# Channel attention on one core: the tensor engine takes the 49 taps two at a time

## The chip, the cores and the metric

The program runs on one NeuronCore of a Trainium2 chip. It is one launch of four layers over a tensor of 4 x 256 x 64 x 64 in float32. The metric is the device time in microseconds, and lower is better. Five engines work side by side, each on its own queue in strict program order: PE (TensorE, with its weight loads), DVE (VectorE), ACT (ScalarE), POOL (GpSimd) and SP (SyncE, which here only issues transfers). They meet at semaphores: an instruction waits until a counter has reached a value, and the instructions behind it on its engine wait with it.

## What is computed

Only layer 2 is touched. For each channel and each pixel it weighs a 7 x 7 window of values by a softmax over the products of the channel's query with the window's keys. There are 49 taps.

```python
def _L2_conv_ref(x, w_q, w_k, w_v, rel_h, rel_w):        # K = 7, PAD = 3
    q = jnp.einsum('bchw,oc->bohw', x, w_q)
    kmap = jnp.einsum('bchw,oc->bohw', x_pad, w_k)
    vmap = jnp.einsum('bchw,oc->bohw', x_pad, w_v)
    kwin = _unfold2d(kmap, K)
    vwin = _unfold2d(vmap, K)
    kwin = jnp.concatenate([kwin[:, :half] + rel_h, kwin[:, half:] + rel_w], axis=1)
    ...
    attn = jax.nn.softmax(q[..., None] * kwin, axis=-1)
    out = jnp.sum(attn * vwin, axis=-1)
    return out
```

The input x is the group-normalised output of layer 1, and `out` is added to it.

## The kernel before

`channel_attention` (line 1395) is a program written by hand: one function per engine lists all its instructions, and semaphores tie the queues. The image is cut into bands of 16 rows, 16 in all (n, counted from 0). A band has four **tiles** (t = 0 to 3) of 128 channels x 512 pixels: `tile_of` makes tiles 0 and 1 of the first half of the channels and tiles 2 and 3 of the second. Each tile runs over 49 **taps** (j). All engines walk through the same order of bands, tiles and taps.

What each engine does for a tap:

- DVE, `multiply` (L1998): key plus relative bias, times the query, into one of three PSUM banks, `stage`. It waits until ACT has emptied that bank, that is for the exponential of three taps ago. Tap 1 of a band's first tile waits for that of tap 48 before it (`bank_lag` 2).
- PE, `shift` (L1679): one matmul of 512 columns with minus the identity takes off the upper bound `top` of the exponents. It waits for the multiply (`multiplied`).
- ACT, `exponential` (L1847): stage to `se` in SBUF. It waits for the shift.
- POOL, `weigh` (L1909): `se` times the window of values into `ev`, 3 or 4 taps in one instruction.
- PE, `sum_exponential` and `sum_weighted` (both through `add_up`, L1686): four transposing matmuls of 128 columns each add a tap of `se` to the bank `pe_sum`, or a tap of `ev` to the bank `pv_sum`. The first comes `E_LAG` = 2 taps behind the shift, the second `V_LAG` = 12 taps.

In between stand works of other tiles. The projections of the next half-band (K1, K2, Q1, Q2 in tiles 0 and 2, V1, V2 in tiles 1 and 3; K0 and V0 only where an image begins) are put on PE by `PROJ_AT`, in two halves g at taps j and j + 1. All use the one bank `pj`. ACT copies each out two taps after its place (L1821), and DVE takes the new keys out of `pj` too (L1946, L1950), to make the running maxima and minima `near` (L1958) from which `ext`, `high` and `top` come (L1974, L1981, L1983). `NEAR` and `EXT_AT` say at which taps.

The end of a tile runs into the next one. ACT takes `pe_sum` after the exponential of tap 1 (`take_e_sums`, L1835), DVE inverts it in four pieces at taps 3, 5, 7 and 9 (L2006), and divides `pv_sum` after its multiply of tap 12 (`divide`, L2014), for which it needs the weighted sum of tap 48. For that reason the weighted sum of tap 0 (`late`) stands behind the shift of tap 12. PE turns the quotient back at tap 20 (`back`, L1720), DVE adds it to x at tap 23 (L2022). ACT places the next tile's query after the exponential of tap 46 (`place_query`, L1828), when all multiplies of the tile are done.

Of the kernel before, what the change touches and what calls it, by code (L numbers as in the profile page):

```python
# [1389 lines left out]
NTAP = K2 * K2  # L1390
# [4 lines left out]
def channel_attention(nc, sems, x_in, coef, x_out, stats, w_t, rel, ident_in, zeros):  # L1395
# [3 lines left out]
    with ctx:  # L1399
# [68 lines left out]
        E_LAG, V_LAG = 2, 12  # L1468
# [22 lines left out]
        def tiles(n, t, per, more):  # L1491

            return n * (TPB * per) + (t * per + more)
# [5 lines left out]
        def parts(H):  # L1499

            return [p for p in ("K0", "K1", "K2", "Q1", "Q2", "V0", "V1", "V2") if opens(H) or p not in ("K0", "V0")]

        def made(H, p=None):

            return sum(len(parts(i)) for i in range(H)) + (parts(H).index(p) + 1 if p else 0)
# [5 lines left out]
        def nears(H, p=None):  # L1511

            last = [x[1:] for x in near_of(H)].index((p, 1, 0)) + 1 if p else 0
            return sum(near_before(i, len(near_of(i))) for i in range(H)) + near_before(H, last)
# [5 lines left out]
        def exts(H, more):  # L1520
            return H * NEXT_ + more
# [27 lines left out]
        def tile_of(t):  # L1549

            return t // 2 % HALVES, t % 2
# [7 lines left out]
        def before(t, j, lag):  # L1559

            back = t * NTAP + j - lag
            return back // NTAP, back % NTAP

        def bank_of(t, j):

            g = t * NTAP + j
            return 1 if g == TPB * NTAP - 1 else g % NST
# [5 lines left out]
        def group_of(j):  # L1573
            o, i = divmod(j, K2)
            return o * len(ROW_PARTS) + (i >= ROW_PARTS[1][0])
# [67 lines left out]
        def _(pe):  # L1643
# [29 lines left out]
            def shift(n, t, j):  # L1673
                h, u = tile_of(t)
                if j == 0:

                    pe.wait_ge(ext_step, exts(n * HALVES + t // 2, TOP_AT[u]))
                pe.wait_ge(multiplied, tiles(n, t, NTAP, j + 1))
                nc.tensor.matmul(stage[:, bank_of(t, j), :], lhsT=minus[:],  # L1679
                                 rhs=top[h][:, u * TPX:(u + 1) * TPX], start=False, stop=True,  # L1680
                                 skip_group_check=True).then_inc(shifted, 1)

            def add_up(acc, src, j):

                for c in range(NBLK2):
                    last = nc.tensor.matmul(acc[:, c * PART:(c + 1) * PART], lhsT=src[:, c * PART:(c + 1) * PART],  # L1686
                                            rhs=ident[:], is_transpose=True, start=j == 0 and c == 0,
                                            stop=j == NTAP - 1, skip_group_check=True)
                return last

            def sum_exponential(n, t, j, first=False):
                o, i = divmod(j, K2)
                if j == 0 and (t or not first):

                    pe.wait_ge(e_taken, tiles(n, t, 1, 0))
                pe.wait_ge(exp_done, tiles(n, t, NTAP, j + 1))
                add_up(pe_sum, se[(t * K2 + o) % NSE][:, i], j).then_inc(e_summed, 1)

            def sum_weighted(n, t, j, first=False):
                g = group_of(j)  # L1700
                i = j % K2 - ROW_PARTS[g % 2][0]
                if j == 0 and (t or not first):

                    pe.wait_ge(divided, tiles(n, t, 1, 0))
                if i == 0:
                    pe.wait_ge(weighted, tiles(n, t, NG2, g + 1))
                add_up(pv_sum, ev[(t * NG2 + g) % NEV][:, i], j).then_inc(v_summed, 1)

            def back(n, t, copies=0, near_=0):
# [10 lines left out]
                    last = nc.tensor.transpose(pj[:, c * PART:(c + 1) * PART], od[:, c * PART:(c + 1) * PART], ident[:])  # L1720
                last.then_inc(turned_back, 1)

            def step(n, t, j, first=False, final=False):
                h, u = tile_of(t)
                late = j == V_LAG
                if not late and (t * NTAP + j >= V_LAG or not first):
                    sum_weighted(n, *before(t, j, V_LAG), first=first)
                shift(n, t, j)
                if t * NTAP + j >= E_LAG or not first:
                    sum_exponential(n, *before(t, j, E_LAG), first=first)  # L1730
                if late:
                    sum_weighted(n, t, 0, first=first)
                H = n * HALVES + t // 2 + 1
                for g in range(HALVES):
                    p = PROJ_AT[u].get(j - g)
                    if H < NH2 and p in parts(H):
                        free = None
                        if p == parts(H)[0] and H >= 2:
                            free = n * TPB + t - 1
                        elif p == "Q1" and n * TPB + t:  # L1740
                            free = n * TPB + t
                        project(H, p, g, free)
                if j == BACK_AT and (t or not first):
                    whole = H < NH2
                    back(n, t - 1, made(H, ("K2", "V2")[u]) if whole else 0, nears(H, "K2") if whole and u == 0 else 0)
# [829 lines left out]
```

## Time and profile before

| | us |
|---|---|
| median of 3 runs | 7987.79 |
| their lowest and highest | 7983.3, 7996.58 |
| the profiled execution | 7993.27 |
| its span | 7991.6 |

The profiled execution lies 5.5 us above the median, and 1.7 us of its time lie outside the span. Busy shares of the span are PE 94%, DVE 71%, POOL 57%, ACT 46%. The busy time of PE counts from the start of a matmul to its modelled end, so that neighbouring matmuls overlap in it; starts tell more than busy times. The slices of the page show the channel attention in the middle of the span, where POOL and DVE stand at 8 tenths and more. A group of the page has a line, an engine, an operation, and the idle time before it with what ended it.

### The profile page before, as it was taken

To read this page: it belongs to the slowest core of one execution; us is meant where nothing else is said; L and a number is where in the kernel's file an instruction comes from. 1 tells how busy PE (TensorE), PEld (TensorE's weight loads), DVE (VectorE), ACT (ScalarE), POOL (GpSimd) and SP (SyncE) were. 2 spreads that over 40 slices of the span, in tenths; PEclk is the share of its full clock that TensorE was granted. 3 is DMA by queue.
4 is the path that set the end of the run, shared out by engine and by line. 5 is a ranking of instruction groups with operands and counts; after the bars stand their busy time and mean duration, and the time that the engine had idled before them with its cause. 6 is when DMAs were issued, how large, how long until landed. Compare 5 with 4: busy or idle time off the path is not lost. (4 is left out here: it accounts for less than half of the span.)

```text
span 7991.6 us, 141890 instructions
## 1 busy us (share of the span) xinstructions
PE 7529.3 (94%) x55106; PEld 6489.6 (81%) x55106; DVE 5666.6 (71%) x8853; ACT 3670.7 (46%) x7040; POOL 4566.2 (57%) x2002
## 2 busy tenths in 40 slices
PE   5999998989998999599999999999999999997999
PEld 4777776879997776388888888888888888886999
DVE  5666665334443555688888888888888888896664
ACT  3655655423332332255555555555555555554222
POOL 3555552023332000388888888888888788886232
PEclk9999998999999999799999999999999999998999
DMA  3111113865557873100000000000000000002452
GB/s 142 61 58 67 60 58 122 282 161 144 144 147 194 234 210 109 29 20 23 27 18 17 20 23 27 18 18 19 24 27 18 17 20 24 27 9 93 138 164 78
DMA packets 633018, 617.21 MB, mean 77 GB/s; under 512 B 465525, under 2 KB 498421, under 8 KB 627174
## 3 DMA queue, kind: packets, MB, share of 16 engines
q1 hardware_dynamic: 581318, 483.44, 21.8%
q0 software_dynamic: 33856, 96.69, 3.3%
q10 hardware_dynamic: 17376, 30.54, 1.0%
q8 instruction: 330, 5.41, 0.3%
q14 instruction: 138, 1.13, 0.0%
HBM read 397.01 MB, written 193.76 MB: 74 GB/s over the span
## 5 line engine op out<-in xcount | busy, mean ns | idle before, releaser
L1909 POOL TENSOR_TENSOR e_ev<-e_se,e_v 128x2048 f32<-128x2048 f32 (+1 forms) x896 | 3307.7, 3712 | 760.6 <-ACT e_se L1847 758.1
L1847 ACT ACTIVATE e_se<-e_stage 128x512 f32<-128x512 f32 x3136 | 1867.8, 597 | 1851.4 <-PE e_stage L1679 1792.9
L1998 DVE SCALAR_TENSOR_TENSOR e_stage<-e_k,e_rl,e_qp 128x512 f32<-128x512 f32 x3136 | 2290.5, 747 | 340.7 <-ACT e_se L1847 285.7
L1686 PE MATMUL e_pe_sum<-e_ident,e_se 128*128 128x128 f32 x12544 | 1880.6, 272 | 16.5 <-ACT e_se L1847 12.3
L1686 PE MATMUL e_pv_sum<-e_ident,e_ev 128*128 128x128 f32 x12544 | 1875.4, 273 | 0.5 <-POOL e_ev L1909 0.5
L1686 PEld LDWEIGHTS e_pe_sum<-e_ident,e_se 128*128 128x128 f32 x12544 | 1550.6, 140 | 259.1 <-ACT e_es L1835 21.8
L1686 PEld LDWEIGHTS e_pv_sum<-e_ident,e_ev 128*128 128x128 f32 x12544 | 1477.2, 140 | 204.6 <-issue 203.2
L1679 PE MATMUL e_stage<-e_top,e_minus 128*128 128x512 f32 x3136 | 1507.8, 481 | 89.2 <-DVE e_stage L1998 85.6
L911 POOL DMA_DIRECT2D agg<-c_ot x384 | 334.6, 874 | 878.7 <-ACT c_ot L989 769.1
L403 POOL TENSOR_TENSOR a_pr<-a_pr,a_rden 128x480 f32<-128x480 f32 x512 | 494.1, 985 | 547.6 <-DVE a_rden L636 547.6
L1679 PEld LDWEIGHTS e_stage<-e_top,e_minus 128*128 128x128 f32 x3136 | 595.5, 190 | 143.6 <-DVE e_stage L1998 99.7
L596 ACT ACTIVATE a_pr<-a_ps,a_nmax 128x240 f32<-128x240 f32 x1024 | 459.3, 460 | 386.7 <-DVE a_nmax L630 386.7
L1974 DVE SCALAR_TENSOR_TENSOR e_ext<-e_near,e_rl,e_ext 128x512 f32<-128x512 f32 x768 | 575.3, 749 | 12.1 <-ACT e_ext L1857 11.4
L948 PE MATMUL c_pa<-c_x_high,c_w_high 128*128 128x448 f32 (+1 forms) x1440 | 522.6, 363 | 33.4 <-DVE c_w_low L1014 33.4
L948 PE MATMUL c_pa<-c_x_low,c_w_high 128*128 128x448 f32 (+1 forms) x1440 | 522.2, 363 | 0.0
L948 PE MATMUL c_pa<-c_x_high,c_w_low 128*128 128x448 f32 (+1 forms) x1440 | 522.0, 363 | 0.0
L630 DVE TENSOR_REDUCE a_nmax<-a_ps 128x2 f32<-128x480 f32 x512 | 312.9, 653 | 292.1 <-PE a_ps L484 285.0
L2294 PE MATMUL f_pc<-f_x_high,f_w_high 128*128 128x256 f32 x1536 | 440.3, 287 | 15.2 <-DVE f_xr L2474 13.0
L1958 DVE TENSOR_REDUCE e_near<-e_pair 128x192 f32<-128x768 f32 (+1 forms) x392 | 438.3, 1118 | 0.5
L2251 POOL TENSOR_TENSOR f_x_low<-f_xt,f_x_high 128x2560 fp32r<-128x2560 f32 x32 | 186.1, 5817 | 439.9 <-ACT f_x_high L2328 408.0
L2294 PE MATMUL f_pc<-f_x_low,f_w_high 128*128 128x256 f32 x1536 | 434.7, 283 | 0.0
L2294 PE MATMUL f_pc<-f_x_high,f_w_low 128*128 128x256 f32 x1536 | 434.1, 283 | 0.0
(175 smaller groups left out, 11567.5 us busy)
## 6 DMA issues: line engine op xcount, KB each, us to landing
qkv<-b_ot SPq DMA_DIRECT2D x120, 512.0 KB, 5.9
c_xt<-qkv SPq DMA_DIRECT2D x384, 160.0 KB, 3.8
agg<-c_ot POOLq DMA_DIRECT2D x384, 160.0 KB, 2.5
f_ws<-in_L_w_sets SPq DMA_DIRECT2D x32, 1152.0 KB, 7.9
a_xb<-in_x SPq DMA_DIRECT2D x24, 768.0 KB, 5.1
a_xr<-in_x SPq DMA_DIRECT2D x32, 512.0 KB, 3.8
x<-a_xr SPq DMA_DIRECT2D x32, 512.0 KB, 2.7
b_xc<-x SPq DMA_DIRECT2D x32, 512.0 KB, 5.8
```

Source lines behind the costliest of these rows:

```text
L403: nc.gpsimd.tensor_tensor(w, w, by, ALU.mult).then_inc(normalised, 1)
L596: last = nc.scalar.activation(pr[P % BUF][:, i, e, :], ps[:, 2 * s + i, e * NK:(e + 1) * NK], ACT.Exp, bias=nmax[P % BUF][:, i, e:e + 1], ...
L911: pool.dma_start(dst, ot[u][:, b]).then_inc(stored[u], 16)
L948: last = nc.tensor.matmul(pa[:, u, r, 0:(last_ - first) * WW].rearrange("p (k c) -> p k c", c=WW), lhsT=w[u][:, dx].rearrange("p o y -> p ...
L1679: nc.tensor.matmul(stage[:, bank_of(t, j), :], lhsT=minus[:], rhs=top[h][:, u * TPX:(u + 1) * TPX], start=False, stop=True, skip_group_che ...
L1686: last = nc.tensor.matmul(acc[:, c * PART:(c + 1) * PART], lhsT=src[:, c * PART:(c + 1) * PART], rhs=ident[:], is_transpose=True, start=j ...
L1847: nc.scalar.activation(se[(t * K2 + o) % NSE][:, i], stage[:, bank_of(t, j), :], ACT.Exp)\
L1909: nc.gpsimd.tensor_tensor(split(ev[(t * NG2 + g) % NEV][:, 0:size]), split(se[(t * K2 + o) % NSE][:, i:i + size]), window(v[h], h, u, o, i ...
L1958: nc.vector.tensor_reduce(grid(near[:, i])[:, first + low:first + low + part, PAD:PAD + WW], pairs, AX.XY, op)\
L1974: nc.vector.scalar_tensor_tensor(rows(ext[:]), win, r[:, o:o + 1], rows(ext[:]), ALU.add, op)\
L1998: nc.vector.scalar_tensor_tensor(rows(stage[:, bank_of(t, j), :]), win, rl[:, h, o:o + 1], rows(qp[:]), ALU.add, ALU.mult).then_inc(multip ...
L2294: last = nc.tensor.matmul(pc[:, m, s], lhsT=w[:, m, s * KW3 + dy, h], rhs=x[u][:, s, h, rows], start=dy == 0 and h == 0 and i == 0, stop=d ...
```

## The change

Only PE's function `step` is written anew. At an even tap it now issues the work of taps j and j + 1: the weighted sum that belongs to j, the shifts of j and j + 1 in a row, the exponential sums of both, and the weighted sum that belongs to j + 1. At an odd tap it issues no such work. Tap 48 stands alone. Tap 12's weighted sum stays behind the shifts. The projection halves and the turning back stay at their taps, and so now follow the pair in which their tap is: both halves that begin at an even tap stand in a row behind the pair, since nothing is issued between them. The number of instructions of every kind is the same, and the other engines' functions are untouched.

```diff
             def step(n, t, j, first=False, final=False):
                 h, u = tile_of(t)
-                late = j == V_LAG
-                if not late and (t * NTAP + j >= V_LAG or not first):
-                    sum_weighted(n, *before(t, j, V_LAG), first=first)
-                shift(n, t, j)
-                if t * NTAP + j >= E_LAG or not first:
-                    sum_exponential(n, *before(t, j, E_LAG), first=first)
-                if late:
-                    sum_weighted(n, t, 0, first=first)
+                taps = [i for i in (j, j + 1) if i < NTAP] if j % 2 == 0 else []
+                late = [i for i in taps if i == V_LAG]
+                for i in taps[:1]:
+                    if i not in late:
+                        weighted_of(n, t, i, first)
+                for i in taps:
+                    shift(n, t, i)
+                for i in taps:
+                    exponential_of(n, t, i, first)
+                for i in taps:
+                    if i in late or i != taps[0]:
+                        weighted_of(n, t, i, first)
```

`weighted_of` and `exponential_of` only hold the old conditions around `sum_weighted` and `sum_exponential`.

PE around tap 12 of tile 1, before. The `ev` buffers hold products, the `se` buffers exponentials; the last four matmuls on `ev1` are the weighted sum of tap 48 of the tile before.

```order
L1686 MATMUL e_pv_sum<-e_ident,e_ev1 128x128 x4
L1679 MATMUL e_stage<-e_top0,e_minus 128x512 [waits e_multiplied]
L1686 MATMUL e_pe_sum<-e_ident,e_se0 128x128 [waits e_exp_done]
L1686 MATMUL e_pe_sum<-e_ident,e_se0 128x128 x3
L1679 MATMUL e_stage<-e_top0,e_minus 128x512 [waits e_multiplied]
L1686 MATMUL e_pe_sum<-e_ident,e_se0 128x128 [waits e_exp_done]
L1686 MATMUL e_pe_sum<-e_ident,e_se0 128x128 x3
L1686 MATMUL e_pv_sum<-e_ident,e_ev2 128x128 [waits e_weighted,e_divided]
L1686 MATMUL e_pv_sum<-e_ident,e_ev2 128x128 x3
L1668 MATMUL e_pj<-e_xb,e_wt 128x512 [waits e_proj_copied]
L1686 MATMUL e_pv_sum<-e_ident,e_ev2 128x128 x4
L1679 MATMUL e_stage<-e_top0,e_minus 128x512 [waits e_multiplied]
```

The three shifts are those of taps 11, 12 and 13. The same place of the changed kernel:

```order
L1686 MATMUL e_pv_sum<-e_ident,e_ev1 128x128 x4
L1679 MATMUL e_stage<-e_top0,e_minus 128x512 [waits e_multiplied] x2
L1686 MATMUL e_pe_sum<-e_ident,e_se0 128x128 [waits e_exp_done]
L1686 MATMUL e_pe_sum<-e_ident,e_se0 128x128 x3
L1686 MATMUL e_pe_sum<-e_ident,e_se0 128x128 [waits e_exp_done]
L1686 MATMUL e_pe_sum<-e_ident,e_se0 128x128 x3
L1686 MATMUL e_pv_sum<-e_ident,e_ev2 128x128 [waits e_weighted,e_divided]
L1686 MATMUL e_pv_sum<-e_ident,e_ev2 128x128 x7
L1668 MATMUL e_pj<-e_xb,e_wt 128x512 [waits e_proj_copied]
L1668 MATMUL e_pj<-e_xb,e_wt 128x512
```

The shift of tap 11 has moved up into the pair before, so the sum of tap 48 stands directly ahead of the shifts of taps 12 and 13; four sums and both halves of V2 follow them.

PE at tap 24 of tile 2, where the first half of Q1 (L1668) is issued, before:

```order
L1679 MATMUL e_stage<-e_top1,e_minus 128x512 [waits e_multiplied]
L1686 MATMUL e_pe_sum<-e_ident,e_se1 128x128 [waits e_exp_done]
L1686 MATMUL e_pe_sum<-e_ident,e_se1 128x128 x3
L1668 MATMUL e_pj<-e_xb,e_wt 128x512 [waits e_added,e_near_step,e_proj_copied]
L1686 MATMUL e_pv_sum<-e_ident,e_ev3 128x128 x4
L1679 MATMUL e_stage<-e_top1,e_minus 128x512 [waits e_multiplied]
L1686 MATMUL e_pe_sum<-e_ident,e_se1 128x128 [waits e_exp_done]
L1686 MATMUL e_pe_sum<-e_ident,e_se1 128x128 x3
L1668 MATMUL e_pj<-e_xb,e_wt 128x512
```

and in the changed kernel:

```order
L1679 MATMUL e_stage<-e_top1,e_minus 128x512 [waits e_multiplied] x2
L1686 MATMUL e_pe_sum<-e_ident,e_se1 128x128 [waits e_exp_done]
L1686 MATMUL e_pe_sum<-e_ident,e_se1 128x128 x3
L1686 MATMUL e_pe_sum<-e_ident,e_se1 128x128 [waits e_exp_done]
L1686 MATMUL e_pe_sum<-e_ident,e_se1 128x128 x3
L1686 MATMUL e_pv_sum<-e_ident,e_ev3 128x128 x4
L1668 MATMUL e_pj<-e_xb,e_wt 128x512 [waits e_added,e_near_step,e_proj_copied]
L1668 MATMUL e_pj<-e_xb,e_wt 128x512
```

The shift of tap 25 now stands ahead of both halves of Q1, where it stood behind the first.

## Rows read from the trace of the kernel before

**Rows 1.** The page: the span, and the group of the shift.

```profile
span 7991.6 us, 141890 instructions
...
L1679 PE MATMUL e_stage<-e_top,e_minus 128*128 128x512 f32 x3136 | 1507.8, 481 | 89.2 <-DVE e_stage L1998 85.6
```

**Rows 2.** Busy time in a stretch: PE, PEld, DVE, ACT, POOL; clock, DMA.

```profile
core 0: us, PE busy (x) PEld busy (x) DVE busy (x) ACT busy (x) POOL busy (x), PEclk, DMA share, GB/s
3700.00:4200.00 500.00, 491.40 (x3670) 427.84 (x3669) 445.41 (x646) 267.43 (x454) 414.63 (x113) 1.00 0.07 21
```

**Rows 3.** Timeline, quiet taps, PE: start, length, engine, line, operation.

```profile
5000.91 0.48 PE L1679 MATMUL e_stage<-e_top,e_minus 128*128 128x512 f32 x1
...
5001.23 0.60 PE L1686 MATMUL e_pe_sum<-e_ident,e_se 128*128 128x128 f32 x4
...
5001.66 0.60 PE L1686 MATMUL e_pv_sum<-e_ident,e_ev 128*128 128x128 f32 x4
...
5002.02 0.48 PE L1679 MATMUL e_stage<-e_top,e_minus 128*128 128x512 f32 x1
```

**Rows 4.** The same timeline, a shift and the multiply three taps on.

```profile
5004.23 0.48 PE L1679 MATMUL e_stage<-e_top,e_minus 128*128 128x512 f32 x1
...
5005.37 0.76 DVE L1998 SCALAR_TENSOR_TENSOR e_stage<-e_k,e_rl,e_qp 128x512 f32<-128x512 f32 x1 [0.22 <-ACT e_se L1847]
```

**Rows 5.** Timeline of layer 1: 512-column matmuls in a row.

```profile
1450.13 0.39 PE L790 MATMUL b_pq<-b_x_low,b_w_high 128*128 128x512 f32 x1
1450.36 0.39 PE L790 MATMUL b_pq<-b_x_high,b_w_low 128*128 128x512 f32 x1
```

**Rows 6.** Timeline, tile 1 of band 5, taps 11 to 13.

```profile
4647.26 0.60 PE L1686 MATMUL e_pv_sum<-e_ident,e_ev 128*128 128x128 f32 x4
...
4647.90 0.69 DVE L2014 TENSOR_TENSOR e_od<-e_pv_sum,e_rs 128x512 f32<-128x512 f32 x1 [0.17 <-PE e_pv_sum L1686]
...
4648.28 0.48 PE L1679 MATMUL e_stage<-e_top,e_minus 128*128 128x512 f32 x1
...
4648.50 1.41 DVE L1998 SCALAR_TENSOR_TENSOR e_stage<-e_k,e_rl,e_qp 128x512 f32<-128x512 f32 x2
...
4650.70 0.48 PE L1679 MATMUL e_stage<-e_top,e_minus 128*128 128x512 f32 x1
```

**Rows 7.** Timeline, the same tile, multiply and shift of tap 45.

```profile
4687.49 0.75 DVE L1998 SCALAR_TENSOR_TENSOR e_stage<-e_k,e_rl,e_qp 128x512 f32<-128x512 f32 x1
...
4688.47 0.48 PE L1679 MATMUL e_stage<-e_top,e_minus 128*128 128x512 f32 x1
```

**Rows 8.** Who waited for whom, in the stage: us, times, longest.

```profile
PE e_stage L1679 <- DVE e_stage L1998: 85.6, 112, 28.3
...
PEld e_pe_sum L1686 <- ACT e_es L1835: 21.8, 57, 0.4
```

**Rows 9.** Timeline, tile 2: K2 copied and used; taps 25 and 26.

```profile
4715.85 0.60 ACT L1821 ACTIVATE e_k<-e_pj 128x512 f32<-128x512 f32 x1
...
4716.48 0.17 DVE L1946 TENSOR_TENSOR e_pair<-e_pj,e_k 128x8 f32<-128x8 f32 x1
...
4725.56 0.74 DVE L1998 SCALAR_TENSOR_TENSOR e_stage<-e_k,e_rl,e_qp 128x512 f32<-128x512 f32 x1
...
4726.84 0.48 PE L1679 MATMUL e_stage<-e_top,e_minus 128*128 128x512 f32 x1
...
4728.83 0.48 PE L1679 MATMUL e_stage<-e_top,e_minus 128*128 128x512 f32 x1
```

**Rows 10.** Timeline, tile 0: K2 copied, multiply 18, its use, shift 18.

```profile
4588.68 0.59 ACT L1821 ACTIVATE e_k<-e_pj 128x512 f32<-128x512 f32 x1
...
4590.48 0.80 DVE L1998 SCALAR_TENSOR_TENSOR e_stage<-e_k,e_rl,e_qp 128x512 f32<-128x512 f32 x1
4591.13 0.73 DVE L1950 TENSOR_TENSOR e_pair<-e_pj,e_k 128x512 f32<-128x512 f32 x1
...
4591.33 0.51 PE L1679 MATMUL e_stage<-e_top,e_minus 128*128 128x512 f32 x1 [0.70 <-DVE e_stage L1998]
```

**Rows 11.** Timeline, tile 0 of band 6: multiply and shift of tap 1.

```profile
4815.05 2.07 DVE L1998 SCALAR_TENSOR_TENSOR e_stage<-e_k,e_rl,e_qp 128x512 f32<-128x512 f32 x3 [0.24 <-ACT e_se L1847]
...
4816.05 0.48 PE L1679 MATMUL e_stage<-e_top,e_minus 128*128 128x512 f32 x1
```

More of the change, by code:

```diff
@@ L1721, in back, with weighted_of, exponential_of @@
                 last.then_inc(turned_back, 1)
+            def weighted_of(n, t, j, first):
+                if t * NTAP + j >= V_LAG or not first:
+                    sum_weighted(n, *before(t, j, V_LAG), first=first)
+            def exponential_of(n, t, j, first):
+                if t * NTAP + j >= E_LAG or not first:
+                    sum_exponential(n, *before(t, j, E_LAG), first=first)
             def step(n, t, j, first=False, final=False):
                 h, u = tile_of(t)
-                late = j == V_LAG
-                if not late and (t * NTAP + j >= V_LAG or not first):
-                    sum_weighted(n, *before(t, j, V_LAG), first=first)
-                shift(n, t, j)
-                if t * NTAP + j >= E_LAG or not first:
-                    sum_exponential(n, *before(t, j, E_LAG), first=first)
-                if late:
-                    sum_weighted(n, t, 0, first=first)
+                taps = [i for i in (j, j + 1) if i < NTAP] if j % 2 == 0 else []
[10 more added lines that the diff above has]
+                        weighted_of(n, t, i, first)
                 H = n * HALVES + t // 2 + 1
```

## The prediction

> **What bounds the kernel now.** I read four views: the busy time by stretch, the timeline tap by tap, the groups with what ended their waits, and the chain that ended last, which stays in the last layer and says nothing of the channel attention. The stage changed holds 3,136 shifts, 16 bands of 4 tiles of 49 taps, in some 4,000 of the 7,992 us [rows 1]. In a stretch of 500 us within it PE is busy 491 us, VectorE 445, POOL 415, ScalarE 267, at a granted clock of 1.00 [rows 2]: PE is the bound, VectorE close behind.
>
> I write s, e, w for the shift, the exponential sum and the weighted sum of a tap on PE, m for its multiply on VectorE, x for its exponential on ScalarE. Where nothing waits, the starts go s to e 0.32 us, e to w 0.43, w to s 0.36 (5000.91, 5001.23, 5001.66, 5002.02): **1.11 us a tap** [rows 3]. I laid all taps over each other by tile: some 2,300 take 1.08 to 1.12 us, and the rest are taps with a projection half beside them (0.88 more: 4726.84 to 4728.83 is 1.99 [rows 9]) or taps where s waits for m.
>
> So the question is how early m is before its s, its **lead**. It is capped: m of tap j+3 waits for x of tap j, and starts 1.14 us after s of tap j (5004.23, 5005.37) [rows 4]; three taps of 1.107 less 1.14 less the 0.76 of m leave 1.42. The floor is 0.05: m from 4590.48 for 0.80, s at 4591.33, after PE had idled 0.70 [rows 10]. In tile 0 (taps 15 to 30) and tile 2 (19 to 24) leads lie near the floor, because VectorE also makes the extremes; elsewhere they swing between 0.1 and 1.4 with one exception of 2 to 3 us behind projections. PE's waits for m add up to only 85.6 us, 28.3 of them one wait ahead of the first tap [rows 8].
>
> **The change, part by part.** Nothing is added or removed; PE's queue is reordered.
>
> *Pure PE time.* Two 512-column matmuls in a row start 0.23 apart (1450.13, 1450.36) [rows 5]. A pair then takes 0.23 + 0.32 + 3 x 0.43 + 0.36 = 2.20 against 2.22: a gain of 0.02, for 24 pairs x 64 tiles 31 us if PE never waits. Bounds: nothing (second shift like the first, 0.25) and twice that. The Trainium skill ("TensorE: Matmul & The Clock Gate", Back-to-back issue gap) gives N / 2.4 + 2.5 ns, 216 ns at 512 columns; the row says 230, and by the page the gain would be some 20 us more.
>
> *The sum of tap 0* waits for ScalarE to take the old exponential sums, once a tile. e of tap 48 to e of tap 0 has two more sums between in pairs, so this wait, 0.38 us at the weight load (21.8 us over 57) and 0.29 in the step [rows 8], goes: up to 19 us. What is late next is m of tap 5.
>
> *The second shift of each pair* stands 0.23 behind the first instead of 1.11, that is 0.88 earlier, with the sums behind it. PE issues in order, so when m is late both sums wait too. It stalls where the old lead was under 0.88 + 0.05. Once stalled, PE is late by that much until VectorE is itself waiting for x again, then the loss stays. Odd taps count; an even tap's s keeps its place. The Trainium skill (same page, What overlaps and what doesn't) says matmuls start and end strictly in order; by that rule nothing fills the stall. The trace agrees as far as it goes: PE idled those 0.70 us with sums queued.
>
> *Tap 13 of tiles 1 and 3.* VectorE divides between m 12 and m 13, and the divide waits for w of tap 48. In the old order w 48 (4647.26) came a step before s 12 (4648.28); its sum is usable 0.64 later, the divide starts at 4647.90, m 13 follows at +0.60, and s 13 is at 4650.70 with ample lead [rows 6]. Now w 48 is the last item before s 12: with s 12 at 0, w 48 is at -0.36, the divide at 0.28, m 13 from 0.88 to 1.63, s 13 at 1.68 instead of 0.23. **1.45 us per tile, 32 tiles: 46 us.** The two sums, the two V2 halves and the next w all stand behind it.
>
> *Tile 2.* Up to tap 10 PE gains 0.4 (tap 0's wait and the pairs). Tap 13 waits 1.15 as above, and a second shift at tap 15 adds 0.2: s 16 is 0.7 late. The copy of K2 follows x 16, so it is 0.7 late, and VectorE, which took it up 0.03 us after its end (4715.85 + 0.60, 4716.48), is now held by that. m 25 then ends at 4725.56 + 0.74 + 0.72, s 25 starts at 4727.07, and behind it now stand two e, two w and both halves of Q1: 0.32 + 0.43 x 3 + 1.74 + 0.36 = 3.71. s 26 comes at 4730.78 against 4728.83 [rows 9]: **1.95 us, 16 tiles: 31 us.**
>
> *Tile 0* is the same place without the copy, which there ends at 4589.27 and is used at 4591.13, 1.9 us spare [rows 10], and with VectorE itself 0.4 ahead: 1.95 - 0.7 - 0.4 = 0.9, 16 tiles: 14 us. Its other waits for m swallow what came in earlier.
>
> *Tails of tiles.* In tile 1 the lowest odd lead is at tap 45: m 4687.49 + 0.75, s 4688.47, so 0.23 [rows 7], a stall of 0.70. In tiles 0 and 2 it is 0.53, a stall of 0.4, of which VectorE gets some 0.3 back because x of an odd tap is up to 0.5 earlier. 16 x (0.7 + 0.1 + 0.1) = 14 us.
>
> *Tile 3 into tile 0.* m of tap 1 waits for x 48, because they share a bank (4815.05 + 0.76, s at 4816.05) [rows 11]. It comes at about the same time, but 0.88 more of PE's work is now behind it: 0.78 us, 15 times, 12 us.
>
> *Add.* At tap 23 of tiles 1 and 3 VectorE waits for the turned output, which now follows the pair 20, 21: 0.14 at s 25, 32 times, 4 us. Pairs outside these places save 7 us.
>
> Sum: 46 + 31 + 14 + 14 + 12 + 4 - 7 = 114, less 3 for the first and the last band, which lack some of these steps: **+111 us**. POOL's queue is not moved, and w takes its product twelve taps late, so nothing there. The profiled execution took 7993.3 us and the median is 7987.8; the sum goes on the median: 8099.
>
> **Rivals.**
> 1. *Stalls are felt only where a wait replaces a wait* (divide, tap 1), while VectorE, freed earlier by x of odd taps, wins back the tiles 0 and 2 and the tails: 46 + 12 - 20 = +38, **8026**. For it: leads are capped by x, and x comes earlier. Against: in tile 0 VectorE never waits for x.
> 2. *Faster*: the second shift's m is always ready, and only PE's own gains count: 31 + 19 = 50, **7938**. It decides at tap 13: it needs m 13 within 0.23 us of s 12, where the rows give 1.63. It also needs leads of 0.93 where there is 0.23. If two shifts in a row were dearer instead, this is gone too.
> 3. *Worse*: a row of two shifts saves nothing (+24 of the gains counted), and the later copies hold VectorE in tile 0 as in tile 2 (16 x 1.05 = 17): **8140**.
> 4. *The change does nothing*: where VectorE bounds, PE's order is indifferent. That would need VectorE's bound all over the stage; at 445 of 500 it isn't: within 0.2%, 7988.
>
> **How the numbers follow.** Forecast 0.76, with its own range of 8065 to 8130; rival 1 0.10, rival 2 0.04, rival 3 0.08, rival 4 0.02. The range of 8 in 10 takes the forecast's and part of rivals 1 and 3: 8045 to 8140. A measurement can tell about 0.2% from no change, 16 us. Slower by more: 0.76 + 0.10 + 0.08 = 0.94; faster by more: 0.04; within: 0.02.
>
> **What would show it.** PE's waits for m on L1679 should go from 86 us to some 230, with a new one of about 1.4 us at tap 13 in each tile; VectorE's divide should wait for w in every tile rather than in half; PE's wait for the taken sums should be gone; two shifts should start 0.23 apart, a quiet pair 2.20. Stage by stage the shift-to-shift time of a band should grow by some 7 us. It is wrong if the multiply of tap 13 is early, or if the tails of the tiles show no waits; if quiet pairs take much less than 2.20, a gain of PE that I have not seen pays for the waits.

## The result, and the profile after

| | before | after |
|---|---|---|
| median, same chip, 4 executions each | 7992.18 | 8143.52 |
| lowest and highest | 7983.3, 7999.19 | 8134.64, 8148.63 |
| ratio, with its 95% interval | | 1.0187 [1.0172, 1.0202] |
| span of the profiled execution | 7991.6 | 8141.2 |
| first to last shift of the stage | 3988.1 | 4132.5 |

The change makes the program 151 us slower. It was forecast at 111 us slower, and 8143.5 lies 3.5 us above the wider range of 8045 to 8140 (13.5 above the forecast's own). The forecast was put on a median of 7987.8; the kernel before has 7992.2 here, so 4.4 us of the miss are the base. The stage accounts for 144.4 us. Some 6 us lie ahead of it: the first shift starts at 3321.3 us instead of 3315.0. In the twelve profiled executions of this study whose work ahead of the first shift is the same, that start lies anywhere from 3308.9 to 3324.8 us. So nothing shows this to be part of the change, and below I read each kernel by the length of its stage, first shift to last. That too is good to some 3 us only: the first tiles of the images at bands 4, 8 and 12 last up to 1.6 us more or less than before even in a kernel whose other tiles agree within 0.15 (e12), and band 0's 2.7.

The page of the kernel after, span and group of the shift, which answer to [rows 1]:

```profile
span 8141.2 us, 141890 instructions
...
L1679 PE MATMUL e_stage<-e_top,e_minus 128*128 128x512 f32 x3136 | 1224.5, 453 | 197.2 <-DVE e_stage L2012 195.0
```

The count is the same, and the idle time ahead of the shift has gone from 89.2 to 197.2 us. The same stretch as in [rows 2], busy time of PE, PEld, DVE, ACT, POOL, then clock and DMA:

```profile
3700.00:4200.00 500.00, 478.37 (x3534) 414.35 (x3533) 429.58 (x620) 242.23 (x435) 399.39 (x109) 1.00 0.07 21
```

All engines do less in the same 500 us (3,534 matmuls, 3,670 before) at the same granted clock of 1.00. No engine has become a new bound; PE waits. Who waited for whom in the stage (us, times, longest), beside [rows 8]:

```profile
PE e_stage L1679 <- DVE e_stage L2012: 195.0, 250, 28.3
...
DVE e_od L2028 <- PE e_pv_sum L1686: 36.7, 36, 1.7
...
PE e_pe_sum L1686 <- ACT e_se L1861: 18.7, 15, 1.2
```

PE's wait for the multiply grew from 85.6 us in 112 waits to 195.0 in 250. The last two lines are VectorE's divide (L2028) waiting for the weighted sum of tap 48, and PE's exponential sum waiting for ScalarE 15 times, once a band. PE's wait for the taken sums, 21.8 us at the weight load in [rows 8], is gone from the list.

Lateness tells where it happens. I took how much longer each tile lasts than in the kernel before, from the start of its first shift to that of the next tile's, as the median over bands 1 to 14:

| us a band | tile 0 | tile 1 | tile 2 | tile 3 | saved by quiet pairs | sum |
|---|---|---|---|---|---|---|
| forecast | 1.78 | 2.29 | 2.05 | 1.59 | -0.44 | 7.27 |
| measured | 2.13 | 2.56 | 2.54 | 1.95 | in the tiles | 9.18 |

Every tile is later than forecast, by 0.27 to 0.49, and the pairs saved nothing (shown below, where the prediction is gone through). Within a tile the lateness builds up as follows (at the shift of the tap named, against the tile's own first shift):

| tap | 2 | 4 | 6 | 12 | 14 | 16 | 20 | 24 | 26 | 30 | 34 | 40 | 42 | 48 |
|---|---|---|---|---|---|---|---|---|---|---|---|---|---|---|
| tile 0 | 0.70 | 0.41 | 0.41 | 0.35 | 1.49 | 2.12 | 1.20 | 1.18 | 2.18 | 1.21 | 1.79 | 1.79 | 1.95 | 2.13 |
| tile 1 | 0.00 | -0.29 | 0.07 | 0.04 | 1.52 | 1.51 | 1.51 | 1.51 | 1.66 | 1.84 | 2.27 | 2.27 | 2.43 | 2.56 |
| tile 2 | 0.00 | -0.29 | -0.29 | -0.35 | 0.75 | 0.94 | 1.62 | 1.68 | 2.23 | 2.22 | 2.20 | 2.20 | 2.37 | 2.54 |
| tile 3 | 0.00 | -0.30 | 0.07 | 0.03 | 1.51 | 1.51 | 1.51 | 1.51 | 1.66 | 1.83 | 1.83 | 1.83 | 1.83 | 1.95 |

### The profile page after: what moved, and what is told of

The parts are those of the page before. It is cut to its first block and busy times, and to the rows that moved or that the text cites. A ratio compares the mean times of both kernels' runs of the same rounds, so it can differ in the third digit from the quotient of the medians.

```text
span 8141.2 us, 141890 instructions
## 1 busy us (share of the span) xinstructions
PE 7565.9 (93%) x55106; PEld 6511.0 (80%) x55106; DVE 5659.2 (70%) x8853; ACT 3560.7 (44%) x7040; POOL 4564.4 (56%) x2002
## 3 DMA queue, kind: packets, MB, share of 16 engines
q14 instruction: 138, 1.13, 0.0%
## 5 line engine op out<-in xcount | busy, mean ns | idle before, releaser
L1861 ACT ACTIVATE e_se<-e_stage 128x512 f32<-128x512 f32 x3136 | 1764.5, 596 | 2016.8 <-PE e_stage L1679 2006.7
L1686 PE MATMUL e_pv_sum<-e_ident,e_ev 128*128 128x128 f32 x12544 | 1683.1, 273 | 0.1
L1686 PE MATMUL e_pe_sum<-e_ident,e_se 128*128 128x128 f32 x12544 | 1633.1, 272 | 18.7 <-ACT e_se L1861 18.7
L1686 PEld LDWEIGHTS e_pe_sum<-e_ident,e_se 128*128 128x128 f32 x12544 | 1466.9, 140 | 201.4 <-ACT e_se L1861 22.2
L1686 PEld LDWEIGHTS e_pv_sum<-e_ident,e_ev 128*128 128x128 f32 x12544 | 1437.7, 140 | 136.0 <-issue 135.3
L1679 PE MATMUL e_stage<-e_top,e_minus 128*128 128x512 f32 x3136 | 1224.5, 453 | 197.2 <-DVE e_stage L2012 195.0
L1679 PEld LDWEIGHTS e_stage<-e_top,e_minus 128*128 128x128 f32 x3136 | 515.5, 190 | 332.2 <-DVE e_stage L2012 297.0
```

The costliest lines, as they stand in the source:

```text
L1861: nc.scalar.activation(se[(t * K2 + o) % NSE][:, i], stage[:, bank_of(t, j), :], ACT.Exp)\
```

## The experiments

All ratios are to the kernel before, run on the same chip; the stage was 3988.1 us before and 4132.5 after. The last four columns are how much longer a tile lasts than in the kernel before, as above.

| kernel | ratio [95%] | stage | t 0 | t 1 | t 2 | t 3 |
|---|---|---|---|---|---|---|
| after | 1.0187 [1.0172, 1.0202] | 4132.5 | 2.13 | 2.56 | 2.54 | 1.95 |
| e1_single_12 | 1.0129 [1.0113, 1.0144] | 4096.8 | 2.12 | 1.40 | 2.53 | 0.82 |
| e3_divide_13 | 1.0118 [1.0102, 1.0133] | 4081.2 | 2.04 | 1.07 | 2.47 | 0.48 |
| e5_single_12_15 | 1.0111 [1.0094, 1.0128] | 4074.4 | 2.13 | 1.42 | 1.28 | 0.83 |
| e6_single_at_q | 1.0157 [1.0140, 1.0174] | 4113.5 | 1.56 | 2.55 | 2.01 | 1.95 |
| e11_single_tail | 1.0152 [1.0136, 1.0167] | 4117.1 | 1.83 | 2.27 | 2.19 | 1.83 |
| e2_pair_at_2 | 0.9987 [0.9978, 0.9996] | 3974.6 | -0.24 | 0.00 | -0.23 | 0.00 |
| e7_light_before | 0.9861 [0.9841, 0.9881] | 3896.9 | -5.08 | -0.19 | -0.67 | -0.18 |
| e8_light_after | 0.9994 [0.9984, 1.0005] | 3994.5 | -3.02 | 1.47 | 0.69 | 1.04 |
| e4_sums_only | 1.0070 [1.0056, 1.0084] | 4041.0 | 0.57 | 1.26 | 0.78 | 0.60 |
| e9_sums_quiet | 1.0018 [1.0009, 1.0027] | 4002.6 | 0.05 | 0.37 | -0.02 | 0.33 |
| e12_sums_quieter | 1.0000 [0.9991, 1.0009] | 3987.6 | -0.09 | 0.03 | -0.06 | 0.00 |
| e10_best | 0.9952 [0.9939, 0.9966] | 3950.9 | -0.25 | -1.36 | -0.22 | -0.33 |

**Tap 13 of tiles 1 and 3.** First the place as it is after, tile 1 of band 5, against [rows 6]: start, length, engine, line, operation, and the idle time ahead with what ended it.

```profile
4701.31 0.60 PE L1686 MATMUL e_pv_sum<-e_ident,e_ev 128*128 128x128 f32 x4
...
4701.67 0.48 PE L1679 MATMUL e_stage<-e_top,e_minus 128*128 128x512 f32 x1
4701.95 0.69 DVE L2028 TENSOR_TENSOR e_od<-e_pv_sum,e_rs 128x512 f32<-128x512 f32 x1 [1.05 <-PE e_pv_sum L1686]
...
4702.56 1.41 DVE L2012 SCALAR_TENSOR_TENSOR e_stage<-e_k,e_rl,e_qp 128x512 f32<-128x512 f32 x2
...
4703.36 0.50 PE L1679 MATMUL e_stage<-e_top,e_minus 128*128 128x512 f32 x1 [1.21 <-DVE e_stage L2012]
...
4703.70 0.71 PE L1686 MATMUL e_pe_sum<-e_ident,e_se 128*128 128x128 f32 x5
```

The weighted sum of tap 48 starts 0.36 us ahead of shift 12, VectorE waits 1.05 for it and divides, and shift 13 comes 1.69 behind shift 12 (the view ends behind the last line, so that it shows five of the eight matmuls). The forecast was 1.68. Two experiments take this away in different ways. The first leaves taps 12 and 13 apart:

```diff
+                if j in (12, 13):
+                    taps = [j]
```

> The changed kernel with taps 12 and 13 taken one at a time, as before the change; all other pairs stay. Theory W (the loss is PE waiting for a late multiply at second shifts, and the largest single wait is at tap 13, where the divide has to wait for the weighted sum of tap 48): tap 13 stops waiting in tiles 1 and 3 (1.5 us, 32 tiles) and partly in tile 2: the time falls by 47 to 60 us, to about 1.012 of before. Rival P (two shifts in a row and the sums in fours cost PE itself something at every pair): one pair in 24 goes, the loss falls by 6 us, to 1.018.

Tiles 1 and 3 lose 1.16 and 1.13 us of lateness, tiles 0 and 2 nothing: 35.7 us of stage in all. That is more than the rival's 6 and less than the 47 to 60 expected: what tile 2 gains at tap 13 it loses again at the second shift of tap 15 (0.93 late at tap 16, as with the pair). Some 0.33 us is left at tap 13, since the pair of taps 10 and 11 still puts the sum of tap 48 directly ahead of shift 12. The second keeps all pairs and takes away what VectorE waits for, by moving the weighted sums and the divide one tap on:

```diff
-        E_LAG, V_LAG = 2, 12
+        E_LAG, V_LAG = 2, 13
-        DIVIDE_AT, BACK_AT, ADD_AT = 12, 20, 23
+        DIVIDE_AT, BACK_AT, ADD_AT = 13, 20, 23
```

> The changed kernel, all pairs kept, with the weighted sums 13 taps behind instead of 12 and the divide at tap 13: so the weighted sum of tap 48 stands ahead of the exponential sums of a whole pair before the divide, and the divide follows the multiply of the second tap of the pair 12, 13. Theory W: PE no longer waits at tap 13, the gain is that of taking taps 12 and 13 singly: 47 to 60 us less than the changed kernel, about 1.012. If instead the place itself is dear (the two V2 halves, the four sums in a row), nothing moves: 1.018.

The same place of this kernel:

```profile
4681.09 1.04 PE L1686 MATMUL e_pv_sum<-e_ident,e_ev 128*128 128x128 f32 x8
...
4681.88 0.71 PE L1679 MATMUL e_stage<-e_top,e_minus 128*128 128x512 f32 x2
4682.16 0.69 DVE L2028 TENSOR_TENSOR e_od<-e_pv_sum,e_rs 128x512 f32<-128x512 f32 x1 [0.59 <-PE e_pv_sum L1686]
```

The two shifts run in a row (x2), since multiply 13 no longer stands behind the divide. Tiles 1 and 3 lose 1.49 and 1.47 us each, and the stage 51.3 us, some 3 of them in tiles 0 and 2. The term of 46 us is shown, in place and in size.

**Tile 2, the copy of K2.** The forecast had this as the largest term after tap 13: a late copy of K2 holds VectorE, and the pair ahead of Q1 makes PE pay. Two pieces of the timeline after, against [rows 9]:

```profile
4772.70 0.60 ACT L1835 ACTIVATE e_k<-e_pj 128x512 f32<-128x512 f32 x1
...
4773.33 0.17 DVE L1960 TENSOR_TENSOR e_pair<-e_pj,e_k 128x8 f32<-128x8 f32 x1 [1.17 <-ACT e_k L1835]
...
4782.40 0.75 DVE L2012 SCALAR_TENSOR_TENSOR e_stage<-e_k,e_rl,e_qp 128x512 f32<-128x512 f32 x1
...
4783.20 0.51 PE L1679 MATMUL e_stage<-e_top,e_minus 128*128 128x512 f32 x1 [0.29 <-DVE e_stage L2012]
...
4784.86 1.92 PE L1668 MATMUL e_pj<-e_xb,e_wt 128*128 128x512 f32 x4
...
4786.97 0.48 PE L1679 MATMUL e_stage<-e_top,e_minus 128*128 128x512 f32 x1
```

VectorE now waits 1.17 us for the copy, where it waited for nothing. Over the bands (medians, against the tile's first shift) the copy is 0.93 us late, its use 0.94, and the multiplies of taps 19 to 27 0.94. Shift 25 follows multiply 25 (4783.15) at once, and with four sums and both halves of Q1 behind it, shift 26 comes 3.77 later; forecast was 3.71. To test the chain I took off its first link only, far ahead of Q1:

```diff
+                if j in (12, 13, 14, 15):
+                    taps = [j]
```

> The changed kernel with taps 12 to 15 taken one at a time. Against the run with only 12 and 13 single this tells whether tile 2 is late because of a chain: second shift at tap 15 late, so tap 16 and the copy of K2 late, so VectorE late, so the second shifts at taps 19 to 25 late. Theory K (that chain): tile 2 ends its first half some 0.9 us late instead of 2.2, tile 0 as before, 16 x 1.3 = 21 us less than with 12 and 13 single: about 1.010 of before. Rival Q (only the last place, tap 25 with both halves of Q1 behind it, decides): tile 2 still ends 2.2 us late, nothing gained, 1.013.

The same use of K2 in that kernel:

```profile
4753.00 0.60 ACT L1837 ACTIVATE e_k<-e_pj 128x512 f32<-128x512 f32 x1
...
4753.66 0.17 DVE L1962 TENSOR_TENSOR e_pair<-e_pj,e_k 128x8 f32<-128x8 f32 x1
```

No wait is left: the copy is 0.36 us early against before instead of 0.93 late. Beside e1, tile 2 falls from 2.53 to 1.28, while tile 0 stays at 2.13, though its shift 16 is 0.45 late there and 2.12 after the change. So the lateness at tap 15 is handed on in tile 2, where the trace shows the copy in between, and not in tile 0, as forecast. The other end of the chain is the pair that stands ahead of the query's projections in tiles 0 and 2:

```diff
+                if u == 0 and j in (24, 25, 30, 31):
+                    taps = [j]
```

> The changed kernel with taps 24, 25, 30 and 31 of tiles 0 and 2 taken one at a time, so that the second shift no longer stands ahead of a projection half that used to run before it. Theory Q: in tiles 0 and 2 the stretch ends 0.6 us a tile or more sooner, 32 x 0.6 = 19 us less than the changed kernel, about 1.016. If the stretch is paid at its earlier taps (K), it moves by less than 5 us: 1.018.

It gives 19.0 us of stage back, as expected: 0.57 in tile 0 and 0.53 in tile 2. With four pairs a band undone it removes only part of what these tiles lose, since VectorE stays late and the next odd taps pay some of it.

**Tails.** Taps 36 to 47 one by one:

```diff
+                if 36 <= j < 48:
+                    taps = [j]
```

> The changed kernel with taps 36 to 47 of every tile taken singly. Theory W: the tails of the tiles lose what they gained in waits (0.34, 0.29, 0.34 and 0.12 us by tile in the changed kernel's trace), 16 x 1.1 = 17 us less than the changed kernel, about 1.0165. Rival: VectorE bounds there, and the wait only moves to the next tile, 1.018.

This gives 15.4 us back: 0.30, 0.29, 0.35 and 0.12 in tiles 0 to 3. It measures the lateness of the tails by taking them away.

**What a pair saves by itself.** The order of before, with the one pair of taps 2 and 3 in each tile (the diffs are on the code after, but for e7's):

```diff
-                taps = [i for i in (j, j + 1) if i < NTAP] if j % 2 == 0 else []
+                taps = [2, 3] if j == 2 else [] if j == 3 else [j]
```

> The kernel before with a single pair per tile, taps 2 and 3. There PE waits 0.29 us a tile for ScalarE to take the old exponential sums, and nothing else is near its limit. Theory W: the wait goes in all 64 tiles, but in tiles 1 and 3 VectorE is the bound up to tap 6 and gives nothing back, so about 32 x 0.29 = 9 us less, 0.999 of before. Rival P: the pair costs more than that wait, not faster than before.

In tiles 0 and 2 it saves 0.24 us: the exponential sum of tap 0 no longer waits for ScalarE. In tiles 1 and 3 the same is won at tap 2 and given back by tap 6, where VectorE's inversions make the multiplies late. So of the 19 us that this wait could give, some 8 arrive in the tiles' medians (0.47 us a band). The stage is 13.5 us shorter; the other 6 lie in the first tile of each image (-2.3 us in bands 4 and 12), where e12 differs by 1.5 us from before as well, and are not explained.

**VectorE made light.** Here the running extremes are made on 8 of the 64 columns of each row only, so the bound of the exponents is another, once on the kernel before and once on the one after:

```diff
-                                ap=[a.ap[0], [PW, part], [1, WW], [3 * away, 2], [2 * away, 2]])
+                                ap=[a.ap[0], [PW, part], [1, 8], [3 * away, 2], [2 * away, 2]])
```

(and the same in two more places).

> The kernel before with VectorE relieved: the reductions that make the near extremes and the additions into ext work on 8 of 64 columns, so the upper bound of the exponents is not the reference's; every instruction, wait and order stays. VectorE no longer bounds tiles 0 and 2: about 6.5 us less a band, some 100 us less than before, 0.987.

> The changed kernel with the same relief of VectorE (8 of 64 columns, the bound of the exponents is not the reference's). Theory W: what is left of the loss is what does not hang on VectorE's load: tap 13 in all tiles (64 x 1.4 = 90), tap 1 of a band (12), tap 34 of tile 1 (6), the add (4), less the wait at tap 2 (19): 93 us more than the relieved kernel before. Rival P (PE pays for the order itself): the whole 144 us stay.

PE's wait for the multiply in the one and in the other (us, times, longest):

```profile
PE e_stage L1679 <- DVE e_stage L2000: 29.9, 18, 17.1
```

```profile
PE e_stage L1679 <- DVE e_stage L2014: 113.3, 117, 17.1
```

The difference of their stages is 97.6 us, where it is 144.4 with VectorE at its full work. 93 were expected. The 47 us that go depended on how busy VectorE is. In the part that stays, the pair of taps 12 and 13 alone makes up 1.1 to 1.5 us in each tile. Tile by tile the pairs cost 2.07, 1.66, 1.35 and 1.22 us here. By the way it shows that seven eighths of the work on the extremes cost the kernel before 5.1 us a band in tile 0.

**Only the sums in twos.** If two shifts in a row are the trouble, the other half of the change should be free. The second shift goes back to its place and the two exponential sums stay together:

```diff
-                for i in taps:
+                for i in taps[:1]:
                     shift(n, t, i)
                 for i in taps:
                     exponential_of(n, t, i, first)
+                for i in taps[1:]:
+                    shift(n, t, i)
```

> Pairs as in the change, but the second shift stands behind the two exponential sums instead of ahead of them: the sums are taken in twos, the shifts are not. By the starts (0.32 + 0.44 + 0.36) the second shift then comes 1.11 us after the first, where it was before the change. Theory W: the waits at second shifts are gone but for tap 13 (0.57 us of it remain, 32 tiles, 18 us), and the wait for the taken exponential sums returns: 1.000 to 1.003 of before. Rival P (sums in twos are dear in themselves): near the changed kernel, 1.015 or more.

It missed: 52.9 us of stage, 3.2 us a band, more than a third of the whole loss without the second shift moved forward. The lateness comes in steps at tap 13 (0.60 in tile 1), tap 34 (0.66) and at taps 15, 25 and 31. In this order the weighted sum of tap 48 still stands right ahead of shift 12, and an exponential sum stands a step early, ahead of a shift that it can hold up (read from the order, and tested by what follows). To see whether the order costs anything where nothing depends on it, I left those taps single:

```diff
+                if j in (12, 13, 14, 15, 24, 25, 30, 31, 32, 33):
+                    taps = [j]
```

> The run with sums in twos and shifts apart measured 1.007 where 1.000 to 1.003 was expected. Its trace puts the rest at taps 13, 15, 25, 31 and 34, where a projection half, the divide or an exponential held back by the normalisation stands behind the pair. Here taps 12 to 15, 24, 25 and 30 to 33 are taken singly besides. Theory W: nothing else costs, within 4 us of the kernel before, 1.000. Rival P (sums in fours cost PE itself): about two thirds of the loss of 53 us in the stage stay, 1.004 or more.

It came out between the two: 14.5 us of stage where 4 or 35 were expected, and 0.37 and 0.33 us remain in tiles 1 and 3. The place, tile 1 of band 5:

```profile
4655.44 0.60 PE L1686 MATMUL e_pv_sum<-e_ident,e_ev 128*128 128x128 f32 x4
...
4655.80 0.48 PE L1679 MATMUL e_stage<-e_top,e_minus 128*128 128x512 f32 x1
...
4656.08 0.69 DVE L2032 TENSOR_TENSOR e_od<-e_pv_sum,e_rs 128x512 f32<-128x512 f32 x1 [0.85 <-PE e_pv_sum L1686]
...
4656.82 0.42 PEld L1686 LDWEIGHTS e_pv_sum<-e_ident,e_ev 128*128 128x128 f32 x4 [0.35 <-DVE e_od L2032]
```

The pair of taps 10 and 11 puts the sum of tap 48 behind shift 11, directly ahead of shift 12. VectorE divides late, and the sum of tap 0, which needs the bank that the divide empties, waits 0.35 for it. It is the remainder that e1 had too. With taps 10 and 11 single as well:

```diff
-                if j in (12, 13, 14, 15, 24, 25, 30, 31, 32, 33):
+                if j in (10, 11, 12, 13, 14, 15, 24, 25, 30, 31, 32, 33):
```

> The last run with sums in twos stayed 14.5 us above before in the stage; its trace shows 0.33 us at tap 13 of tiles 1 and 3, because the pair 10, 11 still puts the weighted sum of tap 48 right ahead of the shift of tap 12. Here taps 10 and 11 are taken singly too. Theory W: those 32 x 0.33 = 11 us go, within 4 us of before in the stage, 1.000 to 1.001. Rival P: they stay, and 1.002 is what sums in fours cost.

```profile
4648.79 0.60 PE L1686 MATMUL e_pv_sum<-e_ident,e_ev 128*128 128x128 f32 x4
...
4649.43 0.69 DVE L2032 TENSOR_TENSOR e_od<-e_pv_sum,e_rs 128x512 f32<-128x512 f32 x1 [0.17 <-PE e_pv_sum L1686]
...
4649.81 0.48 PE L1679 MATMUL e_stage<-e_top,e_minus 128*128 128x512 f32 x1
```

The sum is now a shift earlier (4648.79 to 4649.81 is 1.02), the divide waits 0.17 as in [rows 6], and the ratio is 1.0000. So in the 18 pairs a tile that are left, eight sums in a row cost PE nothing and save nothing; what sums in twos cost in e4 came from the six pairs that stand beside a wait.

**A version that beats both.** Three edits to the order of before: the pair (as in e2) of taps 2 and 3; the inversions moved off the taps at which e2's gain went; and ScalarE's normalisation of the next band, which held up the exponential of tap 31, split into its two halves, six taps apart.

```diff
-        INVERT_AT = (3, 5, 7, 9)
+        INVERT_AT = (3, 6, 8, 10)
-                if t == 1 and j == NORM_AT and not final:
-                    normalise(n + 1)
+                if t == 1 and j in (NORM_AT, NORM_AT + 6) and not final:
+                    normalise(n + 1, [int(j != NORM_AT)])
```

> The kernel before with what the study points to: the pair at taps 2 and 3 alone, which ends PE's wait for the taken exponential sums; the pieces of the inversion at taps 3, 6, 8 and 10 instead of 3, 5, 7 and 9, so that VectorE is not the bound ahead of tap 6 in tiles 1 and 3; and the normalisation of the next band in two halves at taps 30 and 36 of tile 1, so that PE does not wait 1.03 us at tap 34. If each gives what its wait measures: 64 x 0.23 + 15 x 1.03 = 30 us less, 0.996. If the inversion's new places only move the wait: 0.997.

Tile 1, the first half of the normalisation, and the shifts of taps 33 and 34:

```profile
4664.97 1.58 ACT L1784 ACTIVATE e_xb<-e_xb,e_cf 128x1408 f32<-128x1408 f32 x1
...
4667.28 0.48 PE L1679 MATMUL e_stage<-e_top,e_minus 128*128 128x512 f32 x1
...
4668.38 0.48 PE L1679 MATMUL e_stage<-e_top,e_minus 128*128 128x512 f32 x1
```

and the kernel before there, where the normalisation is one block of two:

```profile
4671.84 3.07 ACT L1770 ACTIVATE e_xb<-e_xb,e_cf 128x1408 f32<-128x1408 f32 x2
...
4674.15 0.47 PE L1679 MATMUL e_stage<-e_top,e_minus 128*128 128x512 f32 x1
...
4675.45 0.66 PE L1686 MATMUL e_pe_sum<-e_ident,e_se 128*128 128x128 f32 x4 [0.82 <-ACT e_se L1847]
...
4676.30 0.48 PE L1679 MATMUL e_stage<-e_top,e_minus 128*128 128x512 f32 x1
```

The time from shift 33 to shift 34 falls from 2.15 to 1.10. The stage is 37.2 us shorter than before, and the median 7962.3 against 7996.2 on the same chip; 30 us less were expected. Tile 1 has most of it, 1.36 us a band; I did not run the three edits apart, so their split is read from the lateness only: in tile 1 0.33 us are there by tap 7 and 1.03 more come at tap 34, and tile 3, which has no normalisation, keeps 0.33 where e2 gave its 0.23 back.

## Why the prediction was wrong in size and right in kind

**Right, and tested.** PE works in order, and a second shift moved 0.8 us forward, ahead of its multiply, is what costs. Tap 13: 1.48 measured, 1.45 forecast, removed by two independent edits. The Trainium skill ("TensorE: Matmul & The Clock Gate", What overlaps and what doesn't) has matmuls in strict order of start and end; the trace agrees, for during the 1.21 us ahead of shift 13 PE ran none of the ready sums behind it. Tile 2 by way of the copy of K2: shown by e5 and the wait beside it. Tile 3 into tile 0: 0.70 at tap 2 against 0.78. The add at tap 23: 0.15 against 0.14. The sum of tap 0: the wait is gone, as said.

**Right by two errors that cancel.** The forecast put a second shift that needs no wait 0.23 us behind the first, and the next sum 0.32 behind that. The trace has it the other way round, 0.316 and then 0.235 (shown in the next part). So at tap 13 PE waits 1.37 us beyond the step that a ready shift takes, and not 1.45. But a second shift that PE has waited for holds the next start for longer than a ready one: shift 13 starts at 4703.36 and the sum behind it at 4703.70. That is 0.34 where it is 0.235 without a wait, 0.11 more, and 1.37 + 0.11 is 1.48. It is so at stalls in general: the median over the 383 second shifts that start more than 0.36 behind the first is 0.339.

**Wrong, the gain of a pair.** The forecast took 0.23 us for the second shift from two 512-column matmuls of another layer [rows 5]. A quiet pair of the kernel after, PE only, against [rows 3]:

```profile
4707.55 0.71 PE L1679 MATMUL e_stage<-e_top,e_minus 128*128 128x512 f32 x2
4708.10 1.03 PE L1686 MATMUL e_pe_sum<-e_ident,e_se 128*128 128x128 f32 x8
4708.97 1.04 PE L1686 MATMUL e_pv_sum<-e_ident,e_ev 128*128 128x128 f32 x8
4709.76 0.71 PE L1679 MATMUL e_stage<-e_top,e_minus 128*128 128x512 f32 x2
```

4707.55 to 4709.76 is 2.21, where two taps took 2.21 before (2 x 1.107), and in the quiet stretch of tiles 1 and 3 the lateness stays at 1.51 from tap 14 to 24. The second of the two starts 0.316 behind the first (10th to 50th percentile of the 1,536 pairs 0.313 to 0.316), and the first sum 0.235 behind that. The borrowed 0.23 is thus right for the step behind the second shift. What failed is the balance: this step is 0.08 shorter than the 0.316 it replaces, but one of the two places where a shift follows a weighted sum, 0.355 us, has become a sum behind a sum, 0.435, and that takes the 0.08 back. The forecast's 0.02 came from rows with two decimals, and is no more than their rounding. The bound "nothing" was in the text, as the lower end, and was the value. That is 0.44 us a band, 7 us. The Trainium skill (same page, Back-to-back issue gap) gives 216 ns for 512 columns; neither figure of this place, 316 after transposing sums and 235 ahead of them, is that one, and its 20 us of gain did not come.

**Wrong, the tails.** Forecast 0.1 us in tiles 0 and 2, measured 0.34 in each and 0.12 in tile 3. The step that failed is that VectorE wins 0.3 back: in tiles 0 and 2 the multiplies from tap 38 on are 1.71 and 2.12 late where shift 40 is 1.79 and 2.20 late, so it wins 0.08. Tile 0 after, near tap 35:

```profile
4670.13 0.60 ACT L1861 ACTIVATE e_se<-e_stage 128x512 f32<-128x512 f32 x1 [1.04 <-PE e_stage L1679]
...
4670.62 0.69 ACT L1871 ACTIVATE e_ext<-e_near,e_rl 128x512 f32<-128x512 f32 x1
...
4671.23 0.59 ACT L1861 ACTIVATE e_se<-e_stage 128x512 f32<-128x512 f32 x1
...
4671.86 0.76 DVE L2012 SCALAR_TENSOR_TENSOR e_stage<-e_k,e_rl,e_qp 128x512 f32<-128x512 f32 x1 [0.34 <-ACT e_se L1861]
```

Both shifts of the pair were there, but ScalarE's queue has the opening of `ext` (0.69 us) between their exponentials. So the odd one isn't early, and multiply 38 waits for it. This cause is read, not tested by an edit. Tile 3 was given no tail. Its shift 45 stands 0.34 behind shift 44 instead of 0.316, and with the longer step behind a shift that has waited this costs 0.12. The excess of the three tails is 0.24 + 0.24 + 0.12 = 0.6 us a band, 10 us; e11, which takes the tails of all four tiles away, gives 15.4 back.

**Missed, tap 29.** In tiles 1 and 3, the second shift six taps behind the add stalls and costs 0.18: 0.36 us a band, 6 us. From tap 24 on the multiplies are 1.83 late and PE, after tap 25, only 1.66. The forecast looked at tap 25 only.

**Under-sized, tiles 2 and 0.** In tile 2 the step that failed is a sum. The forecast's own terms for shift 16 are 0.4 gained, 1.15 lost at tap 13 and 0.2 at tap 15, which makes 0.95, and it went on with 0.7. Measured are 0.35, 1.10 and 0.19, and shift 16 is 0.94 late, as are the multiplies that the copy holds. With 0.95 for 0.7 the rest of its working gives 2.20 at tap 26, where 2.23 is measured (2.20 at tap 34). That is 0.25 us a band, 4 us. Tile 0 ended 0.11 above its forecast apart from the tail, 2 us; which of its places has it is open. It has stalls at the odd taps from 13 to 25 but for 17, and at 31, and the forecast went no further than tap 25.

These four make 0.44 + 0.60 + 0.36 + 0.36 = 1.76 us a band, and the last 0.15 is spread over tiles 1 and 3 without a place of its own. Together they are the difference between 9.18 and 7.27, and with it nearly all of the 33 us between +144 and +111 in the stage. The rest of the miss, some 11 us, is the base (4.4) and the time ahead of the stage (some 6), of which the forecast said nothing.

**A cause found that the forecast had inside another.** In tile 1 it gave 0.70 us to tap 45. Measured are 0.43 at tap 34 and 0.29 in the tail, 0.72 in all, so the term is right by chance:

```profile
4727.03 3.06 ACT L1784 ACTIVATE e_xb<-e_xb,e_cf 128x1408 f32<-128x1408 f32 x2
...
4729.99 1.07 ACT L1861 ACTIVATE e_se<-e_stage 128x512 f32<-128x512 f32 x2
...
4730.63 0.66 PE L1686 MATMUL e_pe_sum<-e_ident,e_se 128*128 128x128 f32 x4 [1.24 <-ACT e_se L1861]
...
4731.12 1.04 PE L1686 MATMUL e_pv_sum<-e_ident,e_ev 128*128 128x128 f32 x8
```

The normalisation (3.06 us) holds the exponential of tap 31. Its sum waits 1.24 us, where it waited 0.82 before, and eight weighted sums are queued behind it instead of four. The wait itself isn't new. The kernel before has it in the same 15 bands, and it grew from 12.3 us to 18.7:

```profile
PE e_pe_sum L1686 <- ACT e_se L1847: 12.3, 15, 0.8
```

**Rivals.** Rival 3 had it half right: a row of two shifts saves nothing. Its other half fell, for tile 0 isn't held by the copy (e5 leaves it unchanged), and its 24 us of lost gains measured 7. That its 8140 comes nearest to the measured time is luck. Rival 1, that VectorE wins the rest back, fell: the tails alone cost 15 us. Rivals 2 and 4 fell at tap 13.

**Signs.** PE's waits for the multiply came to 195 us where some 230 were expected; the rest of the loss sits in waits for ScalarE and in multiplies that are late with PE only just behind. VectorE's divide was to wait for the weighted sum in every tile. It waits in half of them, 36 times after and 33 before, but for 36.7 us instead of 8.1: in tiles 0 and 2 multiply 12 ends only 0.05 us ahead of its shift, so that the sum is done when VectorE comes to divide. There the divide and multiply 13 in series behind multiply 12 make the 1.1 us. Two shifts start 0.316 apart and not 0.23, and a band grew by 9.2 us and not 7. That the multiply of tap 13 is late, that the tails have waits, and that a quiet pair gains nothing unseen, came out as forecast.

## What to carry to other kernels

Where one engine is bound and works in order, a batch of its work costs what stands behind each wait, not what the work takes: list for each instruction moved forward the lead of its producer, and for each moved back who waits for it. Here the sums in twos were free where nothing waited beside them (e12, ratio 1.0000) and cost 53 us where something did (e4). With three staging banks the lead was 1.4 us in quiet taps, and moving every second shift 0.8 us forward used it up at the places where the producer has other work. And a gain of 0.02 us worked out from steps of two decimals is inside their rounding: count which steps appear and which go, and take each over many instances, before multiplying by 1,536.

## What the runs showed of the hardware that was not expected

The 512-column shift takes 0.316 us to the start of the next instruction when it follows four transposing sums, whether a sum or a second shift comes next, and 0.235 when it follows another shift; a pair of taps takes 2.21 us in either order. When PE has waited for the multiply it is 0.34 in both places (median 0.339, in the kernel after at second shifts and in the kernel before at single ones), so each stall of a second shift costs 0.1 us beyond its wait. Eight transposing matmuls in a row, of four into each of two buffers' sums, take 0.87 (4708.10 to 4708.97), which is twice 0.435. And the layers ahead of the stage, with the same instructions, ended at times that spread over 16 us between executions (first shift at 3308.9 to 3324.8), for a reason that no run here shows: the length of the stage told more of a change than the whole program's time.
